# Phase 2 of a layernorm, attention and fake-quantized FFN kernel: four row tiles normalized and quantized in a row, then transposed

## The reference

```python
def reference(x, Wk, Wq, Wv, kernel, bias):        # x: (4, 4096, 2048) f32
    xn = layernorm(x)                                # no affine part
    K, Q, V = xn @ Wk.T, xn @ Wq.T, xn @ Wv.T        # 2048 x 2048 each
    probs = softmax(causal(Q @ K.T / sqrt(2048)))
    attn = round((probs @ V) * 1e4) / 1e4
    xq = fake_quant(xn, 8, axis=-1)                  # a scale per row
    kq = fake_quant(kernel, 8, axis=0)
    ffn = fake_quant(relu(xq @ kq + fake_quant(bias)), 8, axis=-1)
    return x + attn + ffn
```

## Time and profile before

| | us |
|---|---|
| median of 2 runs | 6168.14 (6164.8 to 6171.48) |
| profiled execution, its own time | 6168.81 |
| its span on core 0, the slowest | 6167.1 |
| shortest span (core 1) | 6087.7 |

### The profile page before, as it was taken

The page is one execution under the profiler, slowest core; times in us unless marked ns, Lnnn a source line. Parts: engine busy times, 40 slices in busy tenths (PEclk is TensorE's granted clock), DMA queues, the critical chain, the costliest instruction groups (busy, mean ns, idle before and its releaser), DMA issues.

```text
span 6167.1 us, 39319 instructions; the slowest of 8 cores (6087.7 to 6167.1 us)
## 1 busy us (share of the span) xinstructions
PE 4053.3 (66%) x9618; PEld 958.5 (16%) x9801; DVE 1080.4 (18%) x1457; ACT 679.9 (11%) x861; POOL 366.9 (6%) x359
## 2 busy tenths in 40 slices
PE   2778787878777775555555542088467677676776
PEld 0121111212121211111111100022011111111111
DVE  1010100101010102111111115856221111101110
ACT  1011010101010101111111111112000000000010
POOL 1000000000000000000000001400010000000000
PEclk9975666657575757555555555599555555555555
DMA  8010010101010004101010021211434424242413
GB/s 155 12 45 25 32 40 16 46 11 47 10 46 11 31 12 96 33 26 30 25 30 25 16 94 64 75 49 52 150 111 135 119 79 140 72 133 79 133 58 106
DMA packets 226437, 380.70 MB, mean 62 GB/s; under 512 B 78369, under 2 KB 152257, under 8 KB 211905
## 3 DMA queue, kind: packets, MB, share of 16 engines
q1 hardware_dynamic: 198386, 277.45, 14.5%
q0 software_dynamic: 27856, 100.73, 5.9%
HBM read 327.83 MB, written 75.51 MB: 65 GB/s over the span
## 4 chain that ended last, share of the span: by engine, by line
PE 64%; issue 15%; DMA 9%; DVE 6%; ACT 3%; POOL 2%; another core or an unknown queue 1%; SPq 0%; DVEq 0%; ACTq 0%; POOLq 0%
PE pspool L431 20%; PE pspool L932 11%; PE pspool L585 10%; PE pspool L459 9%; DMA pool<-vS 6%; PE pspool L364 5%; PE pspool L1005 5%; PE pspool L797 4%; POOL pool L738 2%; DMA pool<-ktS 1%; DVE pool L565 1%; DVE pool L562 1%; DVE pool L742 1%; DVE pool L536 1%
## 5 line engine op out<-in xcount | busy, mean ns | idle before, releaser
L431 PE MATMUL pspool<-pool 128*128 128x512 bf16 x2000 | 1147.3, 586 | 380.1 <-PE pspool L431 120.4
L932 PE MATMUL pspool<-pool 128*128 128x512 bf16 x1127 | 647.4, 585 | 249.0 <-PE pspool L932 68.5
L364 PE MATMUL pspool<-pool 128*128 128x128 bf16 x1312 | 315.6, 263 | 614.2 <-ACT pool L568 322.7
L1005 PE MATMUL pspool<-pool 128*128 128x512 bf16 x1127 | 529.6, 576 | 240.9 <-DMA pool<-vS 187.7
L585 PE MATMUL pspool<-pool 128*128 128x512 bf16 x1000 | 573.7, 586 | 161.3 <-PE pspool L585 60.4
L459 PE MATMUL pspool<-pool 128*128 128x512 bf16 x2008 | 537.4, 387 | 87.1 <-PE pspool L459 10.1
L797 PE MATMUL pspool<-pool 128*128 128x512 bf16 x1003 | 273.4, 393 | 223.8 <-DMA pool<-nxS 182.3
L431 PEld LDWEIGHTS pspool<-pool 128*128 128x128 bf16 x2048 | 214.4, 105 | 1310.4 <-issue 1308.0
L338 DVE TENSOR_SCALAR pool<-pool 128x1 f32<-128x1 f32 x48 | 7.3, 151 | 2042.7 <-ACT pool L336 2042.7
L435 ACT ACTIVATE pool<-pspool 128x512 bf16<-128x512 f32 x128 | 76.4, 597 | 2032.0 <-PE pspool L431 2020.9
L364 PEld LDWEIGHTS pspool<-pool 128*128 128x128 bf16 x1312 | 134.6, 104 | 798.4 <-issue 787.6
(11 more groups left out here) (115 smaller groups left out, 1731.1 us busy)
## 6 DMA issues: line engine op xcount, KB each, us to landing
pool<-ktS SPq DMA_DIRECT2D x36, 2048.0 KB, 8.3
pool<-vS SPq DMA_DIRECT2D x288, 256.0 KB, 2.7
pool<-emb SPq DMA_DIRECT2D x32, 1024.0 KB, 4.8
pool<-x_own SPq DMA_DIRECT2D x32, 1024.0 KB, 8.3
pool<-fker SPq DMA_DIRECT2D x32, 1024.0 KB, 5.0
ktS<-pool POOLq DMA_DIRECT2D x128, 128.0 KB, 2.2
vS<-pool POOLq DMA_DIRECT2D x32, 512.0 KB, 2.9
out<-pool POOLq DMA_DIRECT2D x16, 1024.0 KB, 9.1
```

The lines of the kernel that those rows point to most:

```text
L364: p.step("PE", lambda e, o=psl, i=sap: e.transpose(o, i, identb), reads=[b_src, b_identb], writes=[bT[half]])
L431: e.matmul(pa, W1[:, E * c + 128 * a:E * c + 128 * a + 128], xnT[:, 512 * c:512 * c + 512], start=st, stop=sp),
L932: st=(c == 0), sp=(c == NCH - 1): e.matmul(pa, qt[par][T][:, 128 * c:128 * c + 128], ktb[ks][:, 512 * c:512 * (c + 1)], start=st, stop=sp),
L1005: st=(kc == 0), sp=(kc == nkc - 1): e.matmul(pv, PT[T][:, 128 * kc:128 * kc + 128], vt[vs_][:, fo:fo + fw], start=st, stop=sp),
```

## The change

The body of the tile loop is cut in two functions. `p2_ln(so)` emits steps 1 to 3 for all four tiles; `p2_transposes(so)` emits steps 4 and 5 for all four tiles. The first block's calls stand ahead of the loop over blocks; those of block `so + 1` stand behind the 16 groups of the Q projection of block `so`. To hold four tiles at once, `xnb2` and `nxb` become `xnb4` and `nxb4` with four tiles each; `nxT` gets two buffers; the separate scratch tile `sqt2` goes (the sums write into the tile of `xnb4` that is about to be filled), and so does the unused `z2`. The scratch columns are now those of the tile (`t` and `4 + t`). `par` is `t` for the quantized tile and `t + 1` for the normalized one.

```diff
-        for so in range(NSO):
+        def p2_ln(so):
             for t in range(4):
                 slot = 4 * so + t
                 sl = slot % 2
+                xn_t = xnb4[:, E * t:E * (t + 1)]
+                nx_t = nxb4[:, E * t:E * (t + 1)]
                 p.dma("SYNC", f"x{sl}", ...)
-                rr, negmr, mm = ln_tile(xd2[sl], b_xd2[sl], xnb2, b_xnb2, sqt2, b_sq2, sl)
-                qg = 2 + sl
+                rr, negmr, mm = ln_tile(xd2[sl], b_xd2[sl], xn_t, b_xnb24[t], xn_t, b_xnb24[t], t)
+                qg = 4 + t
...
-                p.step("ACT", lambda e: e.activation(nxb, r12, AF.Copy, bias=-128.0),
-                       reads=[b_r12], writes=[b_nxb])
-                transpose_chunks(nxb, b_nxb, NCH,
-                                 lambda j: (nxT[:, 512 * j:512 * j + 512], b_nxT[j]),
-                                 evac_cls="ACT")
-                nxT3 = nxT.rearrange("p (c j) -> p c j", j=128)
+                p.step("ACT", lambda e, nx_t=nx_t, t=t: e.activation(nx_t, r12, AF.Copy, bias=-128.0),
+                       reads=[b_r12], writes=[b_nxb4[t]])
+
+        def p2_transposes(so):
+            for t in range(4):
+                slot = 4 * so + t
+                nsl = t % 2
+                transpose_chunks(nxb4[:, E * t:E * (t + 1)], b_nxb4[t], NCH,
+                                 lambda j, nsl=nsl: (nxT[nsl][:, 512 * j:512 * j + 512], b_nxT[nsl]),
+                                 evac_cls="ACT", par=t)
+                nxT3 = nxT[nsl].rearrange("p (c j) -> p c j", j=128)
                 p.dma("GPQ", "nxSp", lambda e, slot=slot, nxT3=nxT3: e.dma_start(
                     out=nxS[slot].rearrange("c p j -> p c j"), in_=nxT3),
-                    reads=[b_nxT1], writes=[b_nxS])
+                    reads=[b_nxT[nsl]], writes=[b_nxS])
                 transpose_chunks(
-                    xnb2, b_xnb2, NCH,
+                    xnb4[:, E * t:E * (t + 1)], b_xnb24[t], NCH,
                     lambda j, t=t: (xnT23[:, 4 * j:4 * j + 4, 128 * t:128 * t + 128],
-                                    b_xnT2[j]))
+                                    b_xnT2[j]), par=t + 1)
+
+        p2_ln(0)
+        p2_transposes(0)
+        for so in range(NSO):
             for a in range(NCH):
                 pa = psA[:, 512 * (a % 2):512 * (a % 2) + 512]
...
+            if so + 1 < NSO:
+                p2_ln(so + 1)
+                p2_transposes(so + 1)
```

More of the change, by code:

```diff
@@ L481, in build_nc @@
         o_xd2 = [al.take(E), al.take(E)]
-        o_xnb2 = al.take(E // 2)
-        o_sq2 = al.take(E // 2)
+        o_xnb4 = al.take(4 * E // 2)
+        o_nxb4 = al.take(4 * E // 2)
         o_xnT2 = al.take(NCH * 512 // 2)
@@ L486, in build_nc @@
         o_ci2 = al.take(E)
-        o_z2 = al.take(E)
         o_f2 = al.take(E)
         o_r12 = al.take(E)
-        o_nxb = al.take(E // 2)
-        o_nxT = al.take(E // 2)
+        o_nxT = al.take(E)
         WQ = cb(o_wq, NCH * E)
         xd2 = [cf(o_xd2[0], E), cf(o_xd2[1], E)]
-        xnb2 = cb(o_xnb2, E)
-        sqt2 = cb(o_sq2, E)
+        xnb4 = cb(o_xnb4, 4 * E)
+        nxb4 = cb(o_nxb4, 4 * E)
         xnT2 = cb(o_xnT2, NCH * 512)
@@ L499, in build_nc @@
         ci2 = cI(o_ci2, E)
-        z2 = cf(o_z2, E)
         f2 = cf(o_f2, E)
         r12 = cf(o_r12, E)
-        nxb = cb(o_nxb, E)
-        nxT = cb(o_nxT, E)
+        nxT = [cb(o_nxT, E), cb(o_nxT + E // 2, E)]
         b_WQ = Buf("WQ", slices=True)
         b_xd2 = [Buf("x2a"), Buf("x2b")]
-        b_xnb2 = Buf("xnb2")
-        b_sq2 = Buf("sq2")
+        b_xnb24 = [Buf(f"xnb24_{i}") for i in range(4)]
+        b_nxb4 = [Buf(f"nxb4_{i}") for i in range(4)]
         b_xnT21 = Buf("xnT2")
@@ L512, in build_nc @@
         b_ci2 = Buf("ci2")
-        b_z2 = Buf("z2")
         b_f2 = Buf("f2")
         b_r12 = Buf("r12")
-        b_nxb = Buf("nxb")
-        b_nxT1 = Buf("nxT")
-        b_nxT = [b_nxT1] * (NCH // 4)
+        b_nxT = [Buf("nxT0"), Buf("nxT1")]
         for c in range(NCH):
@@ L531, in build_nc @@
                     writes=[b_xd2[sl]])
-                rr, negmr, mm = ln_tile(xd2[sl], b_xd2[sl], xnb2, b_xnb2, sqt2, b_sq2, sl)
-                qg = 2 + sl
+                rr, negmr, mm = ln_tile(xd2[sl], b_xd2[sl], xn_t, b_xnb24[t], xn_t, b_xnb24[t], t)
+                qg = 4 + t
                 bqg = b_tiny[qg]
-                am, fx, am2, r127, rrt, biasq = (tiny(qg, i) for i in range(6))
-                p.step("DVE", lambda e, am=am: e.reduce_max(am, xnb2, axis=AX.X, apply_absolute_value=True),
-                       reads=[b_xnb2], writes=[bqg])
+                am, fx, am2, r127, rrt, biasq, thr = (tiny(qg, i) for i in range(7))
+                p.step("DVE", lambda e, am=am, xn_t=xn_t, t=t: e.reduce_max(
+                    am, xn_t, axis=AX.X, apply_absolute_value=True),
+                    reads=[b_xnb24[t]], writes=[bqg])
                 p.step("ACT", lambda e, fx=fx, am=am: e.activation(fx, am, AF.Sign), reads=[bqg], writes=[bqg])
@@ L548, in build_nc @@
                 p.step("DVE", lambda e, rr=rr, rrt=rrt, r127=r127: e.tensor_tensor(rrt, rr, r127, op=ALU.mult),
[L549 to L552, removed]
+                       reads=[b_tiny[t], bqg], writes=[bqg])
+                p.step("DVE", lambda e, mm=mm, biasq=biasq, rrt=rrt: e.tensor_scalar(
+                    biasq, mm, rrt, -1.0, op0=ALU.mult, op1=ALU.mult),
+                    reads=[b_tiny[t], bqg], writes=[bqg])
                 p.step("DVE", lambda e, biasq=biasq: e.tensor_scalar(biasq, biasq, 128.0, None, op0=ALU.add),
```

## The result

| | before | after |
|---|---|---|
| median, us | 6171.38 (10 runs) | 6207.98 (11 runs) |
| profiled execution, its own time | 6168.8 | 6212.0 |
| its span, slowest core | 6167.1 | 6210.4 |

The ratio of the changed kernel to the one before is 1.007, with a 95% interval of 1.0053 to 1.0088: slower by 0.5 to 0.9%, so within 2%. The forecast was 6208.

The account below looks back on a forecast made before the run. No engine fills phase 2's tile stretch, so a chain of dependent steps bounds it. A block is 86.7 + 47.0 + 12.3 = 146.0 us, in all +39.2 on 6168.8: 6208, range 6187 to 6224.

Parts of the forecast that it names:

- Part 1, the place of the calls: Next block's layernorm calls behind the 16 Q groups: ACT's in-order queue hides none of the chain under Q; worth 0.
- Rival E: Phase 2, layernorm does run under Q as far as ACT's gaps allow: up to 260 us hidden, 5948; chance 0.02.
- Part 2, four chains: Layernorm and quantization of a block's four tiles run one after another over ACT and DVE, 4 x 21.7 = 86.7 us.
- Part 3, the train: A block's 32 groups of transposes copied out in a row after the fourth chain: 10.3 us plus 36.7, together 47.0.
- a repeated half: Between a tile's two transpose calls PE refills the same PSUM half: 2.40 us copy to copy, against 1.37 when alternating.
- The remaining 12.3 us to the first Q copy: From a block's last normalized copy to its first Q copy: 12.3 us, unchanged by the change.
- In words: Verbal summary: 5 us of cover lost on three tiles, repeated halves about 4 us a block, early PSUM fill returns 2 to 3.
- Block 0: First block: its 9.49 us ACT wait for the first nxS store goes, so it grows by only 4.8 us.
- nxT: Two buffers for quantized transposes bring nothing outside block 0; one is wanted again 24.4 us after first copy, stores land in 4.8.
- Rival C: More waits in the transposes, from a late nxS store or slower hand-overs: 6218 to 6236 us; chance 0.09.
- The sum: A block takes 146.0 us; +4.8, +11.3, +11.9 and +11.2 for blocks 0 to 3, in all +39.2 us.
- The clock: Transposes and Q in phase 2 stay at granted clock 0.50; the rival, a rise for Q to 6004, had 0.03.

## Why the prediction was right

**Part 1, the place of the calls (0 us).** Right. L334 stands 0.49 us behind the last Q copy in both kernels. That it is the queue's order is shown by the run with the chains between Q copies, where only the order of emission differs from the changed kernel: its blocks sum to 252 us less. Rival E was priced at 3 x 86.7 = 260.

**Part 2, four chains (86.7 us).** 86.6 measured; one spacing in a block is 21.9, where the prediction had 21.7 at most.

**Part 3, the train (47.0 us).** 46.2 measured. PE waited for ACT's copy 20 times, five a block, as the prediction had it. The step across a repeated half was put at 2.40 us and took 2.35 once and 2.42 or 2.43 three times, so this term was right. The three steps between quantized copies were put at 4.28, which was one of block 1's slower rows, and took 4.10 to 4.13 in three tiles; those between normalized copies were put at 4.17 and took 4.08 to 4.15 in four. These two make up the 0.8 us a block by which the forecast of blocks 1 to 3 was high. The remaining 12.3 us to the first Q copy came out as 12.31.

**The loss, taken apart.** The sentence of the prediction that begins with "In words" doesn't fit its own sum: 5 us on three tiles and 4 for the halves, less 2 to 3, is 16 to 17 us a block, where the sum and the runs have 10 to 12. The sum didn't use these terms. The runs give, for blocks 1 to 3, 6.9 to 7.5 us for the order and 3.1 to 4.1 for the halves. The traces of block 1 show the single terms. Copies that stand in nobody's cover take 46.2 us after the change and 24.2 before (4.88, 4.70 and 4.64 in three tiles, 10.02 in the last), 22.0 more. Two things come back. Before, each of the four tiles went 3.7 to 3.8 us from the start of L568 to its first copy, as PE began its transposes only then; after, ACT goes on in 1.8 us each time, 7.9 in all. And the cover had a price of its own: the chain of a tile that began under the copies of the one before took 20.9 to 21.3 us from L334 to L568 in place of 19.8, as L338 stood behind the last L372 in DVE's queue, 3.7 in all:

```profile
2756.04 0.43 DVE L372 COPY pool<-pspool 128x512 bf16<-128x512 bf16 x1 [1.11 <-PE pspool L364]
2756.38 0.14 DVE L338 TENSOR_SCALAR pool<-pool 128x1 f32<-128x1 f32 x1
```

22.0 less 7.9 less 3.7 is the 10.4 of block 1. What came back was sized at 2 to 3 us and is 11.6; its two parts are read from the traces, and no run separates them.

**Block 0.** The wait of 9.49 us went, as expected: 4.0 more instead of some 11; 4.8 was forecast.

**nxT.** Its reason was wrong. The prediction had a buffer wanted again 24.4 us after its first copy; but all stores share one counter, so a copy waits for the store of the tile before it also with two buffers, except at the first use of the second one. In the changed kernel that store is issued 6 to 7 us ahead of the copy and lands in 4.8, so nothing came of it. That the second buffer is worth nothing outside of block 0 is shown by the run with one. Rival C had a late store in the train, and no ACT copy of the changed kernel waits for one. It wasn't worth anything in block 0 either, in the new order, since the first store is issued after the weight loads.

**The sum.** 39.2 forecast, 35.9 in the blocks, 36.6 between the medians. That the median fell on 6208 to the microsecond is luck: the blocks were sized 3.3 us too high, and the sum started from 6168.8, while the median of the kernel before came out at 6171.4 with more runs. The two errors cancel. The prediction also had 123 us as about what a measurement can tell from none; the interval of 0.5 to 0.9% shows that some 11 us are enough.

**The clock.** It stayed at 0.50, so the step held for this kernel. Its reason was too wide, though. It said that trains and Q stretches of this kind stay at 0.50, and left open which of the two did it. Q without its own waits went to 1.00 right behind an unchanged train. The Trainium skill, in "TensorE: Matmul & The Clock Gate", section "What's actually happening", puts the clock down to the engine's activity; by that rule, the trace agrees as far as Q goes: with PE busy for 78% of the stretch it stayed at 0.50, with 99% it was at 1.00. The busy share of the profile doesn't settle it alone, though: the V stretch in the earlier trace rows has 7.80 of 10 us, 78% as well, and is at 1.00. Its matmuls stand 0.37 us apart (27 in 10 us), those of Q with their waits 0.71. Nor did a train open Q, as the prediction read the rule: ahead of the Q that went to 1.00, the train stood at 0.50.

## What to carry to other kernels

Emitting the work of the next block behind the loop of this one overlaps nothing if its first step sits in the same in-order queue as the loop's last copies; ask for each engine which instruction stands ahead, and put the long chain between copies, no more of it in a row than the PSUM buffers can bear. Gathering like steps (all layernorms, then all transposes) removes whatever cover the mixed order gave, so look for starts that lie ahead of the previous tile's last copy before regrouping. Two buffers whose stores share one counter act as one, which shows only when the engines around them get faster. And a price such as "a chain hides under two groups" is tied to the length of a group: once the matmuls lost their waits, the same placement stalled PE for 16 us a chain.

## What was not expected of the hardware

The waits of PE for itself cost far more than the change under study. With them a 128x512 matmul takes 0.71 us from one to the next and the clock stays at 0.50 although the engine is 78% busy; without them 16 take 3.46 us (51.9 us for 15 groups) at 1.00, 0.22 each. Leaving the waits out everywhere took the kernel from 6208 to 3815 us. The transposes stay at 0.50 even without them, but this doesn't show that they must: on core 4 of that run PE is busy for only 14 of 28 us in their train, as ACT's copies wait for stores.
